# A kernel of Strassen-like passes: ScalarE copies four products of every unit, an accumulating transfer adds the former passes' sums, and VectorE makes all low halves

## The chip, the cores and the metric

The kernel runs on one core of a Trainium2 chip. The metric is the device time of one execution in microseconds; lower is better. The names of the engines in the profile are PE (TensorE), PEld (TensorE's weight loads), DVE (VectorE), ACT (ScalarE), POOL (GpSimd) and SP (SyncE, which here only issues DMAs).

## The reference

The input x has 8 batches of 512 rows and 2048 columns, all float32. Each batch goes through a linear layer with a low-rank adapter chosen by its id, then through a second linear layer whose weight is stored as 4-bit codes with a scale for each block of 64, and is added to the result:

```python
x = x + ffn(cond(x, weight, bias, lora_a, lora_b, scaling, adapter_id), codes, absmax, bias2)
# cond: x @ weight.T + bias + scale * (x @ a_sel.T) @ b_sel.T     (rank 16)
# ffn:  y @ w.T + bias2,  w = NF4[codes] * absmax by blocks of 64
```

## The kernel before

**The first stage** (to about 912 us of the profile) dequantises the second weight, multiplies the two weights into one, and writes to DRAM the blocks and block sums of this combined weight (`wc_d`) and of x (`xc_d`). This stage is left as it is by the change.

**The product stage** is a fast matrix multiplication with seven products in place of eight, used on two levels. The outer level has seven passes (index `i`, order `OUTER`), each of which multiplies one outer combination of x with one of the weight. A pass has eight units (`QB`; unit number `u = 8*i + q`), one for each batch, and a unit has seven inner products (`k` from 0 to 6, order `INNER = A11, SS1, S2, S4, S3, A12, A22`). A product is 12 matrix multiplications of 128x512 in float32r, or 24 of half the width in the first four passes (`LOWS`), where 16 columns of the adapter are carried along. Every factor is split into a rounded high part and a low rest, hence three multiplications for each block.

**The weight factors** (`comb[f]`, seven buffers, two halves `c` each) stay for a whole pass. At the border between two passes all seven are replaced: SP issues the loads of factor k as soon as product k of the last unit is done (SS1 has a second buffer and is loaded earlier), ACT rounds each half (`comb_hi`, L1001), and then the rest is made (`comb_lo`). DVE makes the rests of SS1, A11, S2, S4 and S3 (L1324) at the steps that `LO_STEPS` gives by hand; POOL makes those of A12 and A22 (L906). PE waits at the first unit of a pass for both halves of a factor before its product.

**The x factors** are made for every unit: SP loads `xg` (one buffer, L587) for unit u+1 at the top of unit u, when DVE has finished the low halves of unit u. DVE makes four sums of it (`sum_x`: L1355, L1358 at k = 2, L1361 at k = 3, L1363 at k = 4), ACT rounds (L1016), DVE subtracts (`x_lo`, L1374), two at k = 3, two at k = 4, three at k = 5. The low-rank columns go the same way through `a_br` and `a_b` (L1378, L1020, L1382, L1028), with one buffer.

**The sums.** The result of unit u is gathered in `r_sb[u % 2]`, four quarters. In passes 1 to 5 SP first loads the sums of an earlier pass into it (`load_base`, L594, issued at k = 1 of unit u-1 after a wait for the store from that buffer), and DVE adds all seven products to it from PSUM (`add_product`, L1452). In passes 0 and 6 (`fresh`) there is no such load: ACT copies the products `COPIED = (0, 1, 2, 6)` (L1063) and DVE adds the other three. The finished sums go to DRAM from SP (`store_sums`), to `m_d` or, in passes 4 and 5, to the output. In pass 6 the totals of two former passes are also loaded, DVE adds the low-rank product to them (`add_lora_pair`, L1465), and at the end of each unit the sums of all (`add_last` L1472, `add_second_last` L1478, 128x2048 each).

**Order.** All waits are semaphores written by hand; each engine runs its list in order. PE needs a PSUM bank free again (`evacuated`): before product 2 of a unit product 0 must have left, before 3 product 1, before 4 product 2, before 6 product 4. Within a step k, DVE's list is: the adaptor's small sums, `add_product`, the low-rank parts, `sum_x`, `x_lo`, and last `comb_lo`.

Of the kernel before, what the change touches and what calls it, by code (L numbers as in the profile page):

```python
# [6 lines left out]
def adaln_ffn_kernel(  # L7
# [29 lines left out]
    P = 128  # L37
# [137 lines left out]
    def fresh(u):  # L175
        return u < QB or u >= BOTH

    def adds_of(u):
        return 3 if fresh(u) else 8 if u >= LOWS else 7

    def added(u, k):
        before = sum(adds_of(n) for n in range(u))
        if fresh(u):
            return before + k - 2
        return before + k + 1 + (1 if u >= LOWS and k > 4 else 0)

    def copied(u, k):
        return 4 * (u if u < QB else QB + u - BOTH) + COPIED.index(k) + 1

    def lows_before(u):  # L190
        return sum(2 if n < QB else 4 for n in range(u))

    def x_bank(u):
        return 2 + 3 * (u % 2) if u < LOWS else 2 + u % 2

# [7 lines left out]

    def low_load(u, t, m):
        return (2 * (u % 2) + t, (u - LOWS) // 2 + 1) if u < BOTH else (2 * m + t, QB + u - BOTH + 1)
# [3 lines left out]

    BY_GPSIMD, ON_VECTOR = (A12, A22), 10  # L210
# [7 lines left out]
    def half_at(i, f, c):  # L218
        n = halves_of(i).index((f, c)) + 1
        if i and f in BY_GPSIMD:  # L220
            return 4 * (i - 1) + n - ON_VECTOR
        return 2 * NF + ON_VECTOR * (i - 1) + n if i else n
# [18 lines left out]
    LO_STEPS = {-1: [0], 0: [1], 2: [2], 3: [3], 5: [4], 6: [5, 6], 7: [7, 8], 8: [9]}  # L241
# [30 lines left out]
    with ctx:  # L272
# [62 lines left out]
        a_br = at("a_br", 59, [P, 2, 3, QT, R], F32)  # L335
# [74 lines left out]
        s_clo_p = sem("block_low_by_gpsimd")  # L410
# [16 lines left out]
        s_ab = sem("a_b_loaded")  # L427
# [17 lines left out]
        s_rld = [sem(f"base_loaded{i}") for i in range(2)]  # L445
        s_rst = [sem(f"sum_stored{i}") for i in range(2)]
        s_tld = [sem(f"total_loaded{i}") for i in range(2)]
# [20 lines left out]
        def _(sp):  # L468
# [141 lines left out]
            def out_block(q, t, m, h):  # L610
                row = tile_row(q, t, m)
                return o_rows[row:row + P, :].rearrange("p (j c) -> p j c", c=SW)[:, :, h * HW:(h + 1) * HW]

            def store_sums(u, t):
# [3 lines left out]
                elif fresh(u):  # L618
                    sp.wait_ge(s_add, added(u, 4))
                    sp.wait_ge(s_cpy, copied(u, 6))  # L620
                else:
                    sp.wait_ge(s_add, added(u, 6))
                src = r_sb[u % 2][:, t, :, :]
                if i < FINAL:
                    sp.dma_start(m_d[i, q, :, t, :], src.rearrange("p n o -> p (n o)")).then_inc(s_rst[u % 2], 16)
                else:
                    sp.dma_start(out_block(q, t, i - FINAL, 0), src.rearrange("p n (c o) -> p (n c) o", c=2)
                                 ).then_inc(s_rst[u % 2], 16)
# [1266 lines left out]
```

## Time and profile before

| | |
|---|---|
| median of 3 runs | 2107.86 us (2107.43 to 2111.29) |
| the profiled execution | 2105.49 us, of which its span is 2103.7 us |
| mean granted clock of TensorE | 0.985 |
| PE busy in the span | 2016.7 us (96%) |
| DVE, ACT, POOL busy | 1610.5 us (77%), 883.8 us (42%), 118.9 us (6%) |
| DMA | 526.14 MB, mean 250 GB/s |
| time of POOL's rests (L906) | 72.1 us in 24 instructions |

The profile's times are those of one execution on the one core. The busy time of PE is made of matrix multiplications that overlap, so it shows whether PE stood still, and not how fast it was. DMA share 1.00 means that all 16 DMA engines had work all the time. A stretch is given in us from the span's start.

### The profile page before, as it was taken

Reading aid. Unit: us, or ns where it says so; the run is one execution under the profiler, and the core shown is the slowest. Engines: PE = TensorE matmul, PEld = TensorE weight load, DVE = VectorE, ACT = ScalarE, POOL = GpSimd, SP = SyncE. Lnnn points to the kernel's source line nnn. Section 1 sums busy time; section 2 is a strip of 40 time slices with the busy share of each in tenths; the row PEclk is TensorE's granted clock in tenths of the full one; section 3 lists DMA queues with packets and bytes.
Section 4 is the critical chain, followed back from the end, with each engine's and each line's share of the span. In section 5 each row is a group of like instructions: output and inputs, shape, how many; then the busy total and the mean of one; then the engine's idle time right before and its main releaser. Section 6 shows DMA issues by size and latency. Waiting matters only on the chain.

```text
span 2103.7 us, 29439 instructions
## 1 busy us (share of the span) xinstructions
PE 2016.7 (96%) x10880; PEld 1713.2 (81%) x10880; DVE 1610.5 (77%) x2377; ACT 883.8 (42%) x1417; POOL 118.9 (6%) x79
## 2 busy tenths in 40 slices
PE   4899999999999999989999999989999999998997
PEld 4788778788878777889989989989997887886876
DVE  8899879866996465575577787787778778778887
ACT  8655555554555332343442342243242234234332
POOL 5100000000000000000020020020002002002000
PEclk8999999999999999999999999999999999999999
DMA  9778878887888788856478677786877878877876
GB/s 283 244 239 263 256 250 259 254 253 244 264 266 252 244 264 275 256 190 218 166 262 269 217 263 257 250 282 210 271 259 231 275 253 261 260 234 242 279 257 231
DMA packets 406277, 526.14 MB, mean 250 GB/s; under 512 B 22992, under 2 KB 293024, under 8 KB 406008
## 3 DMA queue, kind: packets, MB, share of 16 engines
q1 hardware_dynamic: 402824, 513.23, 75.6%
q0 software_dynamic: 3312, 11.03, 1.6%
q8 instruction: 88, 1.44, 0.3%
q14 instruction: 53, 0.43, 0.1%
HBM read 336.47 MB, written 188.76 MB: 250 GB/s over the span
## 4 chain that ended last, share of the span: by engine, by line
PE 80%; DVE 8%; DMA 5%; issue 3%; SPq 2%; ACT 1%; DVEq 0%; ACTq 0%
PE big L1638 19%; PE big L1640 19%; PE big L1639 19%; PE big L1826 10%; PE big L1824 10%; PE big L1653 2%; DVE comb L1324 2%; DMA rq<-xc_d 1%; PE big L1634 1%; DMA xc_d<-rq 1%; DMA a_br<-a_sel_d 1%; DMA comb_raw<-wc_d 1%; DVE r_sb L1452 1%; DMA code_w<-in_L_ffn_codes_dram 1%; DVE xs L1374 1%
## 5 line engine op out<-in xcount | busy, mean ns | idle before, releaser
L1824 PE MATMUL big<-comb,xs 128*128 128x256 f32 x1920 | 468.9, 282 | 15.0 <-DVE r_sb L1452 13.8
L1638 PE MATMUL big<-wq,tile 128*128 128x512 f32 x1088 | 468.4, 431 | 1.2 <-DVE tile L1259 1.2
L1826 PE MATMUL big<-comb,xs 128*128 128x272 f32 (+1 forms) x1920 | 468.0, 286 | 0.0
L1640 PE MATMUL big<-wq,tile 128*128 128x512 f32 x1088 | 427.2, 393 | 0.0
L1639 PE MATMUL big<-wq,tile 128*128 128x512 f32 x1088 | 426.3, 392 | 0.0
L1824 PEld LDWEIGHTS big<-comb,xs 128*128 128x128 f32 x1920 | 363.9, 190 | 20.1 <-DVE comb L1324 14.7
L1826 PEld LDWEIGHTS big<-comb,xs 128*128 128x128 f32 x1920 | 363.9, 190 | 2.3
L1638 PE MATMUL big<-comb,xs 128*128 128x512 f32 x832 | 332.3, 399 | 21.5 <-DVE r_sb L1452 14.8
L1452 DVE TENSOR_TENSOR r_sb<-big,r_sb 128x512 f32<-128x512 f32 x328 | 225.6, 688 | 149.7 <-PE big L1640 98.5
L1640 PE MATMUL big<-comb,xs 128*128 128x512 f32 x832 | 330.6, 397 | 0.0
L1639 PE MATMUL big<-comb,xs 128*128 128x512 f32 x832 | 330.4, 397 | 0.0
L1638 PEld LDWEIGHTS big<-wq,tile 128*128 128x128 f32 x1088 | 205.3, 189 | 68.0 <-ACT cs L968 3.5
L1640 PEld LDWEIGHTS big<-wq,tile 128*128 128x128 f32 x1088 | 204.9, 188 | 44.9
L1639 PEld LDWEIGHTS big<-wq,tile 128*128 128x128 f32 x1088 | 206.7, 190 | 25.5 <-issue 1.0
L1638 PEld LDWEIGHTS big<-comb,xs 128*128 128x128 f32 x832 | 158.3, 190 | 59.6 <-DVE comb L1324 21.3
L956 ACT CAST tile<-raw 128x1024 fp32r<-128x1024 f32 x136 | 141.7, 1053 | 119.7 <-DMA raw<-in_L_cond_weight_dram 117.7
L1016 ACT CAST xs<-xr 128x512 fp32r<-128x512 f32 x224 | 135.1, 619 | 131.0 <-DVE xr L1363 59.2
L1259 DVE TENSOR_TENSOR tile<-raw,tile 128x1024 fp32r<-128x1024 f32 x136 | 162.2, 1221 | 34.8 <-ACT tile L956 34.5
L1640 PEld LDWEIGHTS big<-comb,xs 128*128 128x128 f32 x832 | 158.2, 190 | 36.4
L1639 PEld LDWEIGHTS big<-comb,xs 128*128 128x128 f32 x832 | 158.4, 190 | 34.9
L906 POOL TENSOR_TENSOR comb<-comb_raw,comb 128x1024 fp32r<-128x1024 f32 x24 | 72.1, 3037 | 1661.1 <-ACT comb L1001 1661.1
L1374 DVE TENSOR_TENSOR xs<-xr,xs 128x512 fp32r<-128x512 f32 x224 | 148.9, 685 | 2.5 <-ACT xs L1016 1.9
(144 smaller groups left out, 2440.7 us busy)
## 6 DMA issues: line engine op xcount, KB each, us to landing
raw<-in_L_cond_weight_dram SPq DMA_DIRECT2D x128, 512.0 KB, 4.5
xg<-xc_d SPq DMA_DIRECT2D x112, 512.0 KB, 5.3
xc_d<-rq SPq DMA_DIRECT2D x26, 1792.0 KB, 7.6
r_sb<-m_d SPq DMA_DIRECT2D x80, 512.0 KB, 4.9
m_d<-r_sb SPq DMA_DIRECT2D x64, 512.0 KB, 6.1
wc_d<-cs SPq DMA_DIRECT2D x31, 896.0 KB, 4.9
tb<-wc_d SPq DMA_DIRECT2D x107, 256.0 KB, 5.0
x_nat<-in_x_dram SPq DMA_DIRECT2D x104, 256.0 KB, 4.0
```

Of the source, the lines that this page charges most:

```text
L906: tt(cw[f][:, ks, LO, 0:SW], cr[f][:, ks, LO, 0:SW], cw[f][:, ks, HI, 0:SW].bitcast(F32), ALU.subtract).then_inc(s_clo_p, 1)
L956: nc.scalar.copy(tile[slot][:, HI, :, :], raw[slot][:, LO, :, :]).then_inc(s_hi, 1)
L1016: nc.scalar.copy(x_slot(u, f)[:, HI, :, :], src).then_inc(s_xhi, 1)
L1259: tt(tile[slot][:, LO, :, :], raw[slot][:, LO, :, :], tile[slot][:, HI, :, :].bitcast(F32), ALU.subtract).then_inc(s_lo, 1)
L1324: tt(comb(i, f)[:, ks, LO, 0:SW], src, comb(i, f)[:, ks, HI, 0:SW].bitcast(F32), ALU.subtract).then_inc(s_clo, 1)
L1374: tt(x_slot(u, f)[:, LO, :, :], src, x_slot(u, f)[:, HI, :, :].bitcast(F32), ALU.subtract).then_inc(s_xlo, 1)
L1452: tt(dst, main(bank, u, k not in (1, 3)), dst, ALU.add).then_inc(s_add, 1)
L1638: nc.tensor.matmul(out_ap, t_hi, m_hi, start=first, stop=False, skip_group_check=onto)
L1639: nc.tensor.matmul(out_ap, t_hi, m_lo, start=False, stop=False, skip_group_check=onto)
L1640: return nc.tensor.matmul(out_ap, t_lo, m_hi, start=False, stop=last, skip_group_check=onto)
L1824: nc.tensor.matmul(big[:, bank, 0:HW], x, w[:, 0:HW], start=begin, stop=end, skip_group_check=not opens)
L1826: ins = nc.tensor.matmul(big[:, bank + 1, 0:wide], x, w[:, HW:HW + wide], start=begin, stop=end, skip_group_check=not opens)
```

## The change

Five things are done at once.

1. ACT copies products 0, 1, 2 and 6 of every unit, DVE adds 3, 4 and 5 onto the copies. The small copy `u_low` also goes from DVE to ACT.
2. `load_base` is gone. When a unit of passes 1 to 5 is complete, POOL issues for each half of `r_sb` a DMA that adds `m_d`'s sums to it (`accum_op=ALU.add`), waits for it, and issues the store, which SP issued before. `r_sb[u % 2]` is free for unit u+2 after these stores; ACT's copy of product 0 waits for that.
3. DVE makes the rests of A12 and A22 as well: four more halves for each border, by `LO_STEPS` at k = 1, 2, 3 and 4 of the first unit, each as the last thing of its step. POOL does no arithmetic in the product stage.
4. `a_b` and `a_br` have two buffers, and their load comes one unit earlier.
5. In the very last unit the low-rank pairs come earlier (at k = 3 and 4), one total has a buffer of its own, and the last sums are made and stored in three pieces, so that after the last product only 128x512 twice is left.

```diff
-    BY_GPSIMD, ON_VECTOR = (A12, A22), 10
-    LO_STEPS = {-1: [0], 0: [1], 2: [2], 3: [3], 5: [4], 6: [5, 6], 7: [7, 8], 8: [9]}
+    LO_STEPS = {-1: [0], 0: [1], 2: [2], 3: [3], 5: [4], 6: [5, 6], 7: [7, 8], 8: [9, 10], 9: [11], 10: [12], 11: [13]}
...
+        total_end = at("total_end", 176, [P, 2, 2, SW], F32)
-        a_b = at("a_b", 59, [P, 2, 3, QT, R], F32R)
+        a_b = [at(f"a_b{i}", kb, [P, 2, 3, QT, R], F32R) for i, kb in enumerate((59, 57))]
...
-            def load_base(u):
-                i, q = divmod(u, QB)
-                sp.wait_ge(s_rst[u % 2], 32 * (u // 2))
-                for t in range(2):
-                    sp.dma_start(r_sb[u % 2][:, t, :, :].rearrange("p n o -> p (n o)"), m_d[BASE_OF[i], q, :, t, :]
-                                 ).then_inc(s_rld[u % 2], 16)
...
@@ load_a(u) @@
-                if u:
-                    sp.wait_ge(s_aside, len(WITH_LOW) * u)
+                if u >= 2:
+                    sp.wait_ge(s_aside, len(WITH_LOW) * (u - 1))
...
@@ SP, top of unit u @@
+                if u and u + 2 < LOWS:
+                    load_a(u + 2)
                 if u + 1 < NU:
                     sp.wait_ge(s_xlo, NF * (u + 1))
                     load_x(u + 1)
-                if 1 <= u <= BOTH:
+                if 1 <= u <= QB:
                     store_sums(u - 1, 1)
...
@@ SP, step k of unit u @@
-                    if k == 1 and QB <= u + 1 < BOTH:
-                        load_base(u + 1)
...
-                if u < BOTH:
+                if u < QB:
                     store_sums(u, 0)
...
@@ POOL @@
-            for i in range(1, NF):
-                for n in range(ON_VECTOR, 2 * NF):
-                    f, c = halves_of(i)[n]
-                    ks = slice(HALF * c, HALF * (c + 1))
-                    pool.wait_ge(s_chi, 2 * NF * i + n + 1)
-                    tt(cw[f][:, ks, LO, 0:SW], cr[f][:, ks, LO, 0:SW], cw[f][:, ks, HI, 0:SW].bitcast(F32),
-                       ALU.subtract).then_inc(s_clo_p, 1)
+            for u in range(QB, BOTH):
+                i, q = divmod(u, QB)
+                if u < QB + 2:
+                    pool.wait_ge(s_rst[u % 2], 32 * (QB // 2))
+                else:
+                    pool.wait_ge(s_rst2[u % 2], 32 * ((u - QB) // 2))
+                for t in range(2):
+                    if t == 0:
+                        pool.wait_ge(s_add, added(u, 5))
+                    else:
+                        pool.wait_ge(s_cpy, copied(u, 6))
+                    pool.dma_start(r_sb[u % 2][:, t, :, :].rearrange("p n o -> p (n o)"), m_d[BASE_OF[i], q, :, t, :],
+                                   accum_op=ALU.add).then_inc(s_base[u % 2][t], 16)
+                for t in range(2):
+                    pool.wait_ge(s_base[u % 2][t], 16 * ((u - QB) // 2 + 1))
+                    src = r_sb[u % 2][:, t, :, :]
+                    if i < FINAL:
+                        pool.dma_start(m_d[i, q, :, t, :], src.rearrange("p n o -> p (n o)")
+                                       ).then_inc(s_rst2[u % 2], 16)
+                    else:
+                        pool.dma_start(out_block(q, t, i - FINAL, 0), src.rearrange("p n (c o) -> p (n c) o", c=2)
+                                       ).then_inc(s_rst2[u % 2], 16)
...
@@ ACT, copy_product(u, 0) @@
+                    elif u >= QB + 2:
+                        act.wait_ge(s_rst2[u % 2], 32 * ((u - QB) // 2))
...
@@ ACT, step k of unit u @@
-                    if k == 0 and u < QB:
+                    if k == 0 and u < LOWS:
                         copy_low(u)
-                    if fresh(u) and k in COPIED:
+                    if k in COPIED:
                         copy_product(u, k)
...
@@ DVE, add_product(u, k) @@
-                if fresh(u):
-                    dve.wait_ge(s_cpy, copied(u, 2))
-                elif k >= 3 and k < 6:
-                    dve.wait_ge(s_add, added(u, {3: 2, 4: 1, 5: 0}[k]))
-                else:
-                    dve.wait_ge(s_rld[u % 2], 32 * ((u - QB) // 2 + 1))
+                dve.wait_ge(s_cpy, copied(u, {3: 2, 4: 1, 5: 0}[k]))
...
+            def add_end(n):
+                u = NU - 1
+                t, cols = TAIL[n]
+                if t == 0:
+                    dve.wait_ge(s_add, added(u, 5))
+                    dve.wait_ge(s_cpy, copied(u, 2))
+                    dve.wait_ge(s_lev, 4 * QB)
+                elif cols.start == 0:
+                    dve.wait_ge(s_cpy, copied(u, 6))
+                first, both, out = (b[:, t, cols, :] for b in (total[u % 2], total_end, r_sb[u % 2]))
+                tt(first, first, out, ALU.add).then_inc(s_end, 1)
+                dve.wait_ge(s_end, 2 * n + 1)
+                tt(out, both, out, ALU.add).then_inc(s_end, 1)
...
+                    if u == NU - 1 and k in (3, 4):
+                        for n in range(2 * (k - 3), 2 * (k - 2)):
+                            add_lora_pair(u, n)
+                    if u == NU - 1 and k == 5:
+                        add_end(0)
+                        add_end(1)
+                    if u == NU - 1 and k == 6:
+                        add_end(2)
```

## Rows read from the trace of the kernel before

**Rows 1.** Windows, product stage; us, busy time by engine, clock, DMA share, GB/s.
```profile
...
1060.00:1085.00 25.00, 20.05 (x133) 18.64 (x132) 22.64 (x27) 15.24 (x22) 11.90 (x4) 0.93 0.88 315
1085.00:1225.00 140.00, 140.00 (x1014) 132.90 (x1013) 99.62 (x182) 39.11 (x88) 0.00 (x0) 1.00 0.72 240
...
1560.00:1592.00 32.00, 26.93 (x143) 22.53 (x142) 30.49 (x34) 18.17 (x25) 12.71 (x4) 0.95 0.96 320
...
1905.00:1940.00 35.00, 27.74 (x109) 21.48 (x108) 26.96 (x30) 18.35 (x25) 10.98 (x4) 0.90 0.72 245
...
912.00:2092.00 1180.00, 1144.40 (x6720) 1009.72 (x6719) 902.65 (x1348) 409.76 (x753) 72.11 (x24) 0.99 0.74 246
...
```

**Rows 2.** Waits of the weight loads, 912 to 2104 us; total, times, longest.
```profile
...
PEld big L1638 <- DVE comb L1324: 19.0, 6, 5.0
...
```

**Rows 3.** Timeline of PE, first border; start, length, instruction, [idle before].
```profile
...
1081.57 0.55 PE L1824 MATMUL big<-comb,xs 128*128 128x256 f32 x1 [4.95 <-DVE r_sb L1452]
...
```

**Rows 4.** Timeline of DVE, the same stretch.
```profile
...
1070.50 2.35 DVE L1324 TENSOR_TENSOR comb<-comb_raw,comb 128x1024 fp32r<-128x1024 f32 x2
...
1075.54 1.99 DVE L1378 TENSOR_TENSOR a_br<-a_br 128x64 f32<-128x64 f32 x1 [2.08 <-DMA a_br<-a_sel_d]
1077.45 3.37 DVE L1324 TENSOR_TENSOR comb<-comb_raw,comb 128x1024 fp32r<-128x1024 f32 x1
...
```

**Rows 5.** Timeline of POOL, the same stretch.
```profile
...
1071.14 11.90 POOL L906 TENSOR_TENSOR comb<-comb_raw,comb 128x1024 fp32r<-128x1024 f32 x4 [871.54 <-ACT comb L1001]
```

**Rows 6.** Timeline of SP's queue, second border.
```profile
...
1231.48 1.18 SPq L569 DMA_DIRECT2D comb_raw<-wi_d  x2
...
1233.82 1.22 SPq L587 DMA_DIRECT2D xg<-xc_d  x2
...
1245.61 0.80 SPq L594 DMA_DIRECT2D r_sb<-m_d  x2
```

**Rows 7.** Tile xg, 1225 to 1250 us: its two loads at that border.
```profile
...
DMA to landing us min/median/max: 8.5/9.2/10.0
```

**Rows 8.** Windows inside the second border.
```profile
...
1216.00:1222.00 6.00, 6.00 (x40) 5.41 (x39) 2.98 (x7) 0.82 (x2) 0.00 (x0) 1.00 1.04 370
...
1240.00:1243.00 3.00, 3.00 (x17) 2.47 (x15) 1.23 (x2) 1.21 (x2) 3.00 (x2) 1.00 1.02 412
...
```

**Rows 9.** DMA issues by line: count, size, median us to landing.
```profile
...
r_sb<-m_d SPq DMA_DIRECT2D x80, 512.0 KB, 4.9
m_d<-r_sb SPq DMA_DIRECT2D x64, 512.0 KB, 6.1
...
xc_d<-x_early POOLq DMA_DIRECT2D x12, 512.0 KB, 6.7
...
```

**Rows 10.** Timeline of DVE in the middle of a pass.
```profile
...
1140.36 0.69 DVE L1452 TENSOR_TENSOR r_sb<-big,r_sb 128x512 f32<-128x512 f32 x1 [2.06 <-PE big L1826]
...
1141.24 0.69 DVE L1355 TENSOR_TENSOR xr<-xg 128x512 f32<-128x512 f32 x1
1142.03 0.69 DVE L1358 TENSOR_TENSOR xr<-xr,xg 128x512 f32<-128x512 f32 x1
...
1143.73 0.68 DVE L1361 TENSOR_TENSOR xr<-xg,xr 128x512 f32<-128x512 f32 x1
1144.33 0.68 DVE L1374 TENSOR_TENSOR xs<-xg,xs 128x512 fp32r<-128x512 f32 x1
...
1160.30 0.69 DVE L1452 TENSOR_TENSOR r_sb<-big,r_sb 128x512 f32<-128x512 f32 x1 [0.93 <-PE big L1826]
...
```

**Rows 11.** Timeline of DVE at the end of the kernel.
```profile
...
2092.61 2.28 DVE L1472 TENSOR_TENSOR total<-total,r_sb 128x2048 f32<-128x2048 f32 x1
...
2096.13 2.29 DVE L1478 TENSOR_TENSOR r_sb<-total,r_sb 128x2048 f32<-128x2048 f32 x1
```

**Rows 12.** Chain that ended last, 2085 to 2104 us; start, length, what.
```profile
...
2091.20 0.24 PE big L1848
...
```

**Rows 13.** Timeline of SP's queue, last border.
```profile
...
1910.64 1.23 SPq L569 DMA_DIRECT2D comb_raw<-wi_d  x2
...
1920.23 1.42 SPq L587 DMA_DIRECT2D xg<-xc_d  x2
...
```

**Rows 14.** Timeline of ACT, last border.
```profile
...
1919.27 0.58 ACT L1063 COPY r_sb<-big 128x512 f32<-128x512 f32 x1
...
1929.33 0.62 ACT L1016 CAST xs<-xg 128x512 fp32r<-128x512 f32 x1 [3.50 <-DMA xg<-xc_d]
...
```

**Rows 15.** Timeline of PE, last border.
```profile
...
1919.99 0.76 PE L1638 MATMUL big<-comb,xs 128*128 128x512 f32 x1 [4.60 <-ACT r_sb L1063]
...
```

More of the change, by code:

```diff
@@ L173, in group_at, with pair_at @@
         return m, r, p, c
-    def fresh(u):
-        return u < QB or u >= BOTH
     def adds_of(u):
-        return 3 if fresh(u) else 8 if u >= LOWS else 7
+        return 4 if LOWS <= u < BOTH else 3
     def added(u, k):
-        before = sum(adds_of(n) for n in range(u))
-        if fresh(u):
-            return before + k - 2
-        return before + k + 1 + (1 if u >= LOWS and k > 4 else 0)
+        return sum(adds_of(n) for n in range(u)) + k - 2 + (1 if LOWS <= u < BOTH and k > 4 else 0)
     def copied(u, k):
-        return 4 * (u if u < QB else QB + u - BOTH) + COPIED.index(k) + 1
+        return 4 * u + COPIED.index(k) + 1
     def lows_before(u):
-        return sum(2 if n < QB else 4 for n in range(u))
+        return sum(2 if n < QB else 3 for n in range(u))
     def x_bank(u):
         return 2 + 3 * (u % 2) if u < LOWS else 2 + u % 2
+    def pair_at(u, n):
+        m, t = divmod(n, 2)
+        return (1 - m, t) if u == NU - 1 else (m, t)
+    TAIL = ((0, slice(0, 2)), (1, slice(1, 2)), (1, slice(0, 1)))
     def z_bank(u):
@@ L426, in adaln_ffn_kernel @@
         s_cpy = sem("product_copied")
-        s_ab = sem("a_b_loaded")
+        s_ab = [sem(f"a_b_loaded{i}") for i in range(2)]
         s_adf = sem("a_b_difference_made")
@@ L840, in _ @@
                             load_low(u + 1, t, m)
-            for m in range(2):
-                store_total(NU - 1, m)
+            for n, (t, cols) in enumerate(TAIL):
+                for m in range(2):
+                    sp.wait_ge(s_end, 2 * n + m + 1)
+                    src = (r_sb[(NU - 1) % 2] if m else total[(NU - 1) % 2])[:, t, cols, :]
+                    sp.dma_start(out_block(QB - 1, t, m, 1)[:, 2 * cols.start:2 * cols.stop, :],
+                                 src.rearrange("p n (c o) -> p (n c) o", c=2)).then_inc(s_out[m], 16)
             for n in range(2):
-                sp.wait_ge(s_rst[n], 32 * (BOTH // 2))
-                sp.wait_ge(s_out[n], 32 * QB)
+                sp.wait_ge(s_rst[n], 32 * (QB // 2))
+                sp.wait_ge(s_rst2[n], 32 * ((BOTH - QB) // 2))
+                sp.wait_ge(s_out[n], 32 * (QB - 1) + 16 * len(TAIL))
         @block.gpsimd
@@ L1019, in a_hi @@
                 act.wait_ge(s_adf, u + 1)
-                nc.scalar.copy(a_b[:, HI, :, :, :], a_br[:, LO, :, :, :]).then_inc(s_abhi, 1)
+                nc.scalar.copy(a_b[u % 2][:, HI, :, :, :], a_br[u % 2][:, LO, :, :, :]).then_inc(s_abhi, 1)
             def place_a(u, f):
@@ L1376, in a_difference @@
             def a_difference(u):
[L1377 to L1378 removed]
+                low, high, apart = (a_br[u % 2][:, LO, h, :, :] for h in range(3))
+                dve.wait_ge(s_ab[u % 2], 16 * (u // 2 + 1))
+                tt(apart, high, low, ALU.subtract).then_inc(s_adf, 1)
             def a_lo(u):
                 dve.wait_ge(s_abhi, u + 1)
[L1382 removed]
+                tt(a_b[u % 2][:, LO, :, :, :], a_br[u % 2][:, LO, :, :, :], a_b[u % 2][:, HI, :, :, :].bitcast(F32),
                    ALU.subtract).then_inc(s_ablo, 1)
@@ L1775, in evacuated @@
             def evacuated(u, k):
[L1776 removed]
+                if k in COPIED:
                     pe.wait_ge(s_cpy, copied(u, k))
@@ L1790, in multiply @@
                 if q == 0:
-                    pe.wait_ge(s_clo_p if i and f in BY_GPSIMD else s_clo, max(half_at(i, f, c) for c in range(2)))
+                    pe.wait_ge(s_clo, max(half_at(i, f, c) for c in range(2)))
                 if u < LOWS and f in WITH_LOW:
```

91 lines of the change are left out of this document (42 added, 49 removed).

## The prediction

> **What bounds the kernel now.** I read the windows of the product stage first, since the change touches nothing before it. In the middle of a pass PE is busy all the time: 140.0 of 140 us, at clock 1.00, with DVE at 99.6 us and ACT at 39.1 us of it [rows 1]. A unit takes 1160.30 - 1140.36 = 19.94 us there, a product 2.85 us [rows 10]. So nothing that ACT or DVE saves in mid-pass moves the end. From 912 to 2092 us PE stands still for 1180 - 1144.4 = 35.6 us, and the windows that lie over the borders show where: 4.95 us in the first, 5.07 in the fourth, 7.26 in the last [rows 1]; the other three read alike, and the six have some 33 us. After such a wait the granted clock falls from 2.4 to 1.2 GHz for a while: the first border's window has a mean of 0.93, which is 0.07 x 25 = 1.8 us more [rows 1]. Then comes the tail: the last matmul ends at 2091.4 us, DVE at 2098.4, the span at 2103.7 [rows 11, 12].
>
> Next, why PE waits at a border. The weight loads wait for DVE's rests, 19.0 us in six waits on one of the lines alone [rows 2]; at the first border it is one wait of 4.95 us, before the product with S3 [rows 3]. DVE's own timeline has the reason. Two halves take it 2.35 us in a row, but the next one takes 3.37 us and a small difference 1.99 us, after a wait of 2.08 us for `a_br` [rows 4]. These long ones lie inside POOL's four subtractions from 1071.14 to 1083.04 us [rows 5]: both engines are slow while both work. So today's stall is DVE's, made longer by POOL.
>
> **The change, term by term.**
>
> *Mid-pass.* Four additions less on DVE (0.60 us each from start to start, as 1143.73 to 1144.33 in rows 10) and four copies more on ACT: hidden under PE both ways, 0. ACT has 101 of 140 us free. The copy of product 0 is needed before product 2 begins, 2.85 us after product 0 ends, and takes 0.58 us [rows 14]. 0.
>
> *DVE at a border.* Gone are POOL's grip (1.17 us for a half where rows 4 show 3.37), the wait for `a_br`, and 4 x 0.60 = 2.4 us of additions per unit; new are four halves, 4 x 1.17 = 4.7 us. The S3 half that stops PE today will be ready in time. I read this as: the stall of today goes. What is late next? In DVE's list the second half of A22 now stands last in k = 4 of the first unit, behind `sum_x` and `x_lo` for the next unit, and these wait for `xg`. At the second border the unit begins at about 1231.5 (SP's load of A22 waits for the end of product 6), SP issues xg in two parts from 1233.82 [rows 6], and they take up to 10.0 us to land [rows 7]: 1234.4 + 10.0 = 1244.4, that is 12.9 us into the unit. From there DVE has, by the distances of rows 4 and 10: two sums 1.4, second half of A12 1.17, the addition 0.6, a sum 0.6, two `x_lo` 1.2, first half of A22 1.17, small parts 0.1, the addition 0.6, a sum 0.6, two `x_lo` 1.2, second half of A22 1.17; sum 9.8 us. So A22 is complete 22.7 us into the unit, and PE wants it at 6 x 2.85 = 17.1. A stall of 5.6 us, in the place of today's 5. In passes 4 and 5 `add_lora` stands in that list too: 6.3 us.
>
> *What the transfers do to that landing.* The DMA engines are full around a border: share 1.04 at 1216 to 1222 and 1.02 still at 1240 to 1243 us, at 370 to 412 GB/s [rows 8]. Ahead of xg in that burst stand today the base load of the coming unit (2 x 512 KB) and half of the last unit's store (512 KB). After the change they are gone from SP's queue, but the stores of the unit before come later and fall into the burst (1 MB), and the two accumulating transfers of the last unit stand in it at its worst moment. No row has an accumulating transfer. Lower bound: the load of the same size, 4.9 us; upper bound: a load and a store one after the other, 4.9 + 6.1 = 11.0 us, since it has to read `r_sb` besides writing it [rows 9]. A plain transfer of POOL's takes 6.7 [rows 9]. So the burst ahead of xg changes by +0.5 MB (priced as a load) to +1.5 MB (twice that): at 387 GB/s, the mean between 370 and 412 rounded down, 1.4 to 4.1 us later. I take 2, since a part of POOL's queue will still be running after xg. A gain is possible too, see the rivals. In the first border there is no accumulating transfer yet, and the base load of unit 8 is gone: 1.05 MB / 387 GB/s = 2.7 us earlier, stall 5.6 - 2.7 = 2.9 us.
>
> What would a page make of it? The Trainium skill, "DMA: Bandwidth & Descriptors", section "Rules for kernel authors", says that an accumulating DMA reads its destination and writes it later. By that rule the upper of the two prices is the nearer, and the borders would cost 2 us each more than I write; no row here can show it.
>
> *The last border.* PE stops for 4.60 us for ACT's copy, which comes at 1919.27, and resumes at 1919.99 [rows 14, 15]; before the copy ACT's list holds roundings whose loads SP issued as late as 1910.64 [rows 13]. The change leaves this as it is. xg is issued at 1920.23 [rows 13] and used at 1929.33 after a wait [rows 14]; + 9.8 is 1939.1. Without a further wait PE would reach product 6 at 1920.0 + 4 x 2.85 + 1.7 (low clock) = 1933.1. So 4.6 + 6.0 = 10.6 us, and 1 for the fuller DMA: 11.6, where today it is 7.3 [rows 1].
>
> *Sum of the borders*: 2.9 + 2 x 7.6 + 2 x 8.3 + 11.6 = 46.3 us against 33: +13. The low clock comes after each wait before and after: 0.
>
> *The r_sb buffer.* POOL's chain for a unit begins with the copy of product 6, 0.7 us after the unit's end: accumulate, store (6.1), two issues of about 1 us. ACT wants the buffer 19.94 + 2.85 = 22.8 us after that end, so the accumulation may take 22.8 - 0.7 - 2 - 6.1 = 14 us. Both bounds (4.9 and 11.0) fit: 0, with the price below if not.
>
> *SP* issues less (0.8 us for two base loads, [rows 6]) and waits less; it is not what PE waits for in mid-pass: 0.
>
> *The tail.* Today, after the last matmul: 2.28 + 1.15 + 2.29 us of additions with their gaps, end at 2098.4, and 5.3 us to the end of the span [rows 11]. Afterwards: a copy of 0.6, two additions of 0.6 and 0.7, so the end at 2091.4 + 2.0 = 2093.4, and 5.0 for a smaller store: 2098.4. -5.3 us.
>
> Sum: +13 - 5.3 = +7.7 us on the profiled execution's own 2105.5, 2113.2. The median of the runs shown lies 2.4 us above that execution, so 2115.6; I say 2115.
>
> **The rivals.**
>
> *A, faster: SP's queue gets through sooner.* xg stands behind 1.5 MB less in its own queue. If POOL's transfers take little from the engines while SP's queue is full, xg lands up to 1.55 MB / 387 GB/s = 4 us earlier, and the stalls become 2.9, 2 x 1.6, 2 x 2.3 and about 8: 19 us, so -14, and stalls under 3 us may keep the clock: about -5. With the tail -24: 2083. For it: DVE is free of POOL, and the median landing of POOL's plain transfers, 6.7, is slow. Against: full DMA engines [rows 8] serve both queues. The Trainium skill, "DMA: Bandwidth & Descriptors", section "Queues, rings and completion order", has each DMA engine take turns between the queues that have work; by that POOL's part comes at once and A gets nothing.
>
> *B, no difference: the accumulation costs as little as the load.* Then xg lands as today: 2.9 + 2 x 5.6 + 2 x 6.3 + 10.6 = 37.3, +4, less the tail 5.3: -1, 2107.
>
> *C, much slower: the accumulation is longer than 14 us.* Then ACT's copy of product 0 waits for POOL's store, and ACT holds up PE in mid-pass too. It decides from 14 us for ACT and 17 for PE; at 23 us it would cost (23 - 17) / 2 = 3 us for each of about 38 units, +114: 2220. Both bounds speak against it.
>
> **How the numbers follow.** Forecast 0.42 (2109 to 2126), A 0.30, B 0.20, C 0.08. A measurement of this kernel tells about 0.2% (4.2 us) from no change. Faster by more: A and a little of B, 0.34. Within: most of B and the lower edge of the forecast, 0.22. Slower: 0.44. The range takes in A down to 2080 and the forecast with the price of the accumulation doubled again (five borders by 4 us) up to 2145; half of A's low side and C are outside, under 0.2.
>
> **What would show it.** In the trace after: PE without idle time in mid-pass; at each border one wait, no longer before S3 but before A22 (product 6), released by DVE's L1324 group, with DVE waiting for xg shortly before; halves at 1.22 us throughout; accumulating transfers of 5 to 11 us; xg landing 9 to 12 us after its issue; the span's end about 12.3 - 5.3 = 7 us behind the last matmul. The prediction is wrong if xg lands early (A), if ACT's copies wait for POOL's stores (C), or if DVE reaches k = 4 late for another reason than xg.

## Result, and the profile after

The changed kernel takes 2158.09 us (median; 2155.66 to 2159.74), the kernel before 2107.66 (2107.43 to 2111.29) beside it: ratio 1.0239, 95% interval 1.0227 to 1.0252. It is slower, as the forecast's sign had it, but by 50 us where the prediction had 8; the time is outside the range.

The page of the changed kernel, then windows of its product stage (busy time of PE, PEld, DVE, ACT, POOL, then clock, DMA share, GB/s):

```profile
PE 2035.0 (94%) x10880; PEld 1727.1 (80%) x10880; DVE 1495.2 (69%) x2221; ACT 975.5 (45%) x1601; POOL 167.6 (8%) x215
...
q1 hardware_dynamic: 367528, 429.33, 61.8%
q0 software_dynamic: 26352, 94.93, 17.2%
```

```profile
940.00:1060.00 120.00, 120.00 (x869) 113.92 (x869) 70.01 (x120) 47.94 (x106) 0.00 (x0) 1.00 0.60 199
1066.00:1096.00 30.00, 24.77 (x164) 23.34 (x163) 23.20 (x34) 16.38 (x28) 0.94 (x1) 0.89 0.56 189
1100.00:1210.00 110.00, 110.00 (x794) 104.27 (x793) 62.14 (x113) 41.43 (x95) 14.79 (x21) 1.00 0.82 244
1214.00:1268.00 54.00, 44.54 (x288) 41.41 (x288) 35.95 (x54) 26.69 (x47) 6.07 (x9) 0.91 0.77 237
...
1950.00:2000.00 50.00, 34.16 (x118) 25.95 (x117) 33.32 (x43) 22.53 (x31) 3.27 (x4) 0.83 0.67 222
912.00:2146.00 1234.00, 1161.01 (x6703) 1022.73 (x6703) 788.22 (x1188) 500.65 (x936) 120.96 (x160) 0.97 0.77 235
```

In the middle of pass 1 PE still never stops (110.00 of 110 us), though the DMA share is 0.82 where it was 0.72 [rows 1]: the moved copies and additions are hidden. From 912 us to the end of the stage PE stands still for 1234 - 1161.01 = 73.0 us, where it was 35.6, nearly all at the borders; a border's clock is 0.83 to 0.91, where it was 0.90 to 0.95 [rows 1]. By the trace's clock records the time at 1.2 GHz grows from 27.3 to 71.7 us, and half of each such us at most is lost: up to 22 us. The last matmul of the kernel before, then of the changed one:

```profile
2091.65 0.40 PE L1848 MATMUL big<-g_b,low_st 128*128 128x512 f32 x1
```

```profile
2149.70 0.39 PE L1669 MATMUL big<-comb,xs 128*128 128x512 f32 x1
```

It ends at 2092.05 and at 2150.09 us, 58.0 us later. Of these 37.4 are standing still, and 20.6 are PE longer busy with the same matmuls, which fits the low clock. The spans end 11.6 us (2103.7) and 7.5 us (2157.6) behind these ends: -4.1. Together +53.9, the distance of the spans.

**The first border.** PE's timeline, then DVE's:

```profile
1082.78 0.39 PE L1853 MATMUL big<-comb,xs 128*128 128x256 f32 x1 [1.22 <-DVE comb L1338]
...
1089.94 0.58 PE L1853 MATMUL big<-comb,xs 128*128 128x256 f32 x1 [4.00 <-DVE comb L1338]
```

```profile
1074.01 2.35 DVE L1338 TENSOR_TENSOR comb<-comb_raw,comb 128x1024 fp32r<-128x1024 f32 x2
1076.81 0.36 DVE L1397 TENSOR_TENSOR a_b<-a_br,a_b 128x192 fp32r<-128x192 f32 x1 [0.45 <-ACT a_b L1032]
1080.10 0.69 DVE L1369 TENSOR_TENSOR xr<-xg 128x512 f32<-128x512 f32 x1 [2.93 <-DMA xg<-xc_d]
...
1081.51 1.22 DVE L1338 TENSOR_TENSOR comb<-comb_raw,comb 128x1024 fp32r<-128x1024 f32 x1
...
1085.05 1.22 DVE L1338 TENSOR_TENSOR comb<-comb_raw,comb 128x1024 fp32r<-128x1024 f32 x1
...
1088.67 1.22 DVE L1338 TENSOR_TENSOR comb<-comb_raw,comb 128x1024 fp32r<-128x1024 f32 x1
```

This is the predicted wait at the predicted place: the stall before S3 [rows 3] is gone, halves take 1.22 us, and PE stops before product 6 until the last half of A22 (1088.67 + 1.22). Ahead of it DVE had stood still for `xg` for 2.93 us. Such a wait before product 6 stands at each of the six borders: 4.00, 3.21, 2.67, 5.14, 4.61 and 4.03 us, 23.7 in sum.

**The second border**, unit 15, the last of pass 1. From here on accumulating transfers run beside the burst. PE, ACT and DVE:

```profile
1235.85 0.55 PE L1853 MATMUL big<-comb,xs 128*128 128x256 f32 x1 [3.96 <-DVE r_sb L1457]
```

```profile
1228.96 1.05 ACT L1013 CAST comb<-comb_raw 128x1024 fp32r<-128x1024 f32 x1 [4.73 <-DMA comb_raw<-wc_d]
```

```profile
1230.05 1.23 DVE L1338 TENSOR_TENSOR comb<-comb_raw,comb 128x1024 fp32r<-128x1024 f32 x1 [4.02 <-ACT comb L1013]
1231.19 0.68 DVE L1457 TENSOR_TENSOR r_sb<-big,r_sb 128x512 f32<-128x512 f32 x1
...
1235.02 0.68 DVE L1457 TENSOR_TENSOR r_sb<-big,r_sb 128x512 f32<-128x512 f32 x1
```

This wait the prediction did not have. Read backwards: product 6 waits for the addition of product 4 (1235.02), which stands in DVE's list behind a rest of A11's weights, which waits for ACT's rounding, which waits for the load. PE also waits in the last units of passes 2 and 3 (4.56 and 5.24 us, there seen at the transposes on L1801). The rest of A11 waits for ACT there too, for 2.06 and 1.77 us, but the sums of `xg` ahead of it had waited for their load first, 2.10 and 8.98 us, so late loads of both kinds share in these. The wait comes, in those of passes 4 and 5 (1.90 and 2.01). The four parts of that load, from issue to landing, first in the kernel before, where they were issued from 1214.4 us:

```profile
L561 SPq DMA_DIRECT2D comb_raw<-wc_d x4: 370/510/1210, 1214.4 to 1216.7; - x4
...
DMA to landing us min/median/max: 4.7/5.6/6.6
```

and in the changed one, from 1217.7 us:

```profile
L563 SPq DMA_DIRECT2D comb_raw<-wc_d x4: 370/714/982, 1217.7 to 1219.7; - x4
...
DMA to landing us min/median/max: 9.6/10.2/10.9
```

What ran beside them is in POOL's timeline: two accumulating transfers issued just ahead. The stores behind them wait for their landing, so the first took at most 5.7 us and the second at most 11.1:

```profile
1213.51 0.87 POOL L909 DMA_DIRECT2D r_sb<-m_d  x1 [6.70 <-DVE r_sb L1457]
1215.74 0.87 POOL L909 DMA_DIRECT2D r_sb<-m_d  x1 [1.36 <-ACT r_sb L1077]
1219.17 0.56 POOL L915 DMA_DIRECT2D m_d<-r_sb  x1 [2.56 <-DMA r_sb<-m_d]
1226.87 0.54 POOL L915 DMA_DIRECT2D m_d<-r_sb  x1 [7.14 <-DMA r_sb<-m_d]
```

**The last border** has the longest stop. ACT's copy stands behind roundings that wait for late loads:

```profile
1971.30 0.76 PE L1667 MATMUL big<-comb,xs 128*128 128x512 f32 x1 [6.34 <-ACT r_sb L1077]
1977.75 0.47 PE L1667 MATMUL big<-comb,xs 128*128 128x512 f32 x1 [1.53 <-ACT r_sb L1077]
1986.39 0.50 PE L1667 MATMUL big<-comb,xs 128*128 128x512 f32 x1 [1.94 <-DVE comb L1338]
1993.47 0.80 PE L1667 MATMUL big<-comb,xs 128*128 128x512 f32 x1 [4.03 <-DVE comb L1338]
```

**All transfers**, by line: count, size, median us to landing.

```profile
xg<-xc_d SPq DMA_DIRECT2D x112, 512.0 KB, 6.8
...
r_sb<-m_d POOLq DMA_DIRECT2D x80, 512.0 KB, 8.3
...
m_d<-r_sb POOLq DMA_DIRECT2D x48, 512.0 KB, 7.0
comb_raw<-wi_d SPq DMA_DIRECT2D x44, 512.0 KB, 9.8
comb_raw<-wc_d SPq DMA_DIRECT2D x83, 256.0 KB, 8.8
```

Accumulating takes 8.3 us where the load took 4.9 [rows 9], and everything beside it lands later: xg 6.8 (5.3 before), the two kinds of loads of weights 9.8 and 8.8 (7.6 and 6.3 before).

### The profile page after: what moved, and what is told of

The parts are those of the page before. It is cut to its first block, busy times and chain, and to the rows that moved or that the text cites. A ratio compares the mean times of both kernels' runs of the same rounds, so it can differ in the third digit from the quotient of the medians.

```text
span 2157.6 us, 29402 instructions
## 1 busy us (share of the span) xinstructions
PE 2035.0 (94%) x10880; PEld 1727.1 (80%) x10880; DVE 1495.2 (69%) x2221; ACT 975.5 (45%) x1601; POOL 167.6 (8%) x215
## 3 DMA queue, kind: packets, MB, share of 16 engines
q0 software_dynamic: 26352, 94.93, 17.2%
## 4 chain that ended last, share of the span: by engine, by line
PE 73%; DMA 10%; DVE 9%; issue 3%; SPq 3%; ACT 1%; DVEq 0%; ACTq 0%
PE big L1667 18%; PE big L1669 18%; PE big L1668 18%; PE big L1855 7%; PE big L1853 7%; DMA xg<-xc_d 6%; PE big L1682 2%; DVE xs L1388 2%; DMA comb_raw<-wc_d 2%; DVE comb L1338 1%; DMA rq<-xc_d 1%; SPq L563 1%; PE big L1663 1%; DVE r_sb L1457 1%; DMA low_d<-low_st 1%
## 5 line engine op out<-in xcount | busy, mean ns | idle before, releaser
L1853 PE MATMUL big<-comb,xs 128*128 128x256 f32 x1920 | 479.0, 286 | 25.0 <-DVE comb L1338 13.4
L1855 PE MATMUL big<-comb,xs 128*128 128x272 f32 (+1 forms) x1920 | 477.2, 290 | 0.0
L1853 PEld LDWEIGHTS big<-comb,xs 128*128 128x128 f32 x1920 | 371.2, 193 | 30.1 <-DVE comb L1338 16.4
L1855 PEld LDWEIGHTS big<-comb,xs 128*128 128x128 f32 x1920 | 371.2, 193 | 2.4
L1077 ACT COPY r_sb<-big 128x512 f32<-128x512 f32 x224 | 131.6, 587 | 353.5 <-PE big L1669 213.0
L1667 PEld LDWEIGHTS big<-comb,xs 128*128 128x128 f32 x832 | 159.6, 192 | 72.6 <-DVE comb L1338 30.3
L1669 PEld LDWEIGHTS big<-comb,xs 128*128 128x128 f32 x832 | 159.5, 192 | 37.0
L1668 PEld LDWEIGHTS big<-comb,xs 128*128 128x128 f32 x832 | 159.8, 192 | 35.1
L1273 DVE TENSOR_TENSOR tile<-raw,tile 128x1024 fp32r<-128x1024 f32 x136 | 162.2, 1220 | 35.5 <-ACT tile L968 35.4
L909 POOL DMA_DIRECT2D r_sb<-m_d x80 | 70.3, 887 | 1312.4 <-DVE r_sb L1457 1241.7
```

What stands on the lines that cost most here:

```text
L909: pool.dma_start(r_sb[u % 2][:, t, :, :].rearrange("p n o -> p (n o)"), m_d[BASE_OF[i], q, :, t, :], accum_op=ALU.add).then_inc(s_base[u % ...
L1077: nc.scalar.copy(quarter_of(r_sb[u % 2], t, n), main(bank, u, k != 1)).then_inc(s_cpy, 1)
L1273: tt(tile[slot][:, LO, :, :], raw[slot][:, LO, :, :], tile[slot][:, HI, :, :].bitcast(F32), ALU.subtract).then_inc(s_lo, 1)
L1667: nc.tensor.matmul(out_ap, t_hi, m_hi, start=first, stop=False, skip_group_check=onto)
L1668: nc.tensor.matmul(out_ap, t_hi, m_lo, start=False, stop=False, skip_group_check=onto)
L1669: return nc.tensor.matmul(out_ap, t_lo, m_hi, start=False, stop=last, skip_group_check=onto)
```

## The experiments

Two questions: how much is the order of VectorE's list, how much are the transfers; and are the two independent? In e1, e2, e10 and e11 the kernel leaves out a part of the result, as each expectation says; they serve as measurements alone. Each run stood beside runs of the kernel before (medians 2107.0 to 2108.2); the ratios are to those. "Still" is PE's time without work from 912 us to the end of the stage, "low" the time at 1.2 GHz, of all clock records that reach into it, counted whole. Both are of the profiled execution, "us" is the median of all.

| run | us | ratio, 95% | still | low |
|---|---|---|---|---|
| before | 2107.7 | 1 | 35.6 | 27.3 |
| changed | 2158.1 | 1.0227 to 1.0252 | 73.0 | 71.7 |
| e1 plain load | 2134.1 | 1.0096 to 1.0145 | 60.6 | 58.0 |
| e2 no base | 2118.0 | 1.0021 to 1.0053 | 43.8 | 37.5 |
| e3 before, rests on VectorE | 2122.2 | 1.0042 to 1.0085 | 43.8 | 37.5 |
| e4 before, last unit changed | 2103.6 | 0.9973 to 0.9996 | 37.1 | 27.3 |
| e5 A22 early | 2122.6 | 1.0053 to 1.0093 | 50.4 | 44.4 |
| e6 and A11 late | 2128.0 | 1.0071 to 1.0112 | 54.6 | 34.1 |
| e7 old sums, two a_b | 2103.5 | 0.9967 to 0.9989 | 35.4 | 30.7 |
| e8 and rests on VectorE, early | 2097.8 | 0.9932 to 0.9967 | 29.7 | 37.5 |
| e9 lists eased | 2135.4 | 1.0103 to 1.0143 | 55.9 | 64.9 |
| e10 eased, plain load | 2103.1 | 0.9964 to 0.9990 | 35.0 | 37.5 |
| e11 eased, no base | 2082.8 | 0.9869 to 0.9900 | 20.1 | 20.5 |
| e12 old sums, eased | 2090.1 | 0.9901 to 0.9932 | 27.1 | 17.1 |

**e1 and e2: the transfers, in the changed kernel's own lists.** e1 drops `accum_op`; e2 drops the transfers of the former sums altogether.

```diff
                     pool.dma_start(r_sb[u % 2][:, t, :, :]..., m_d[BASE_OF[i], q, :, t, :],
-                                   accum_op=ALU.add).then_inc(s_base[u % 2][t], 16)
+                                   ).then_inc(s_base[u % 2][t], 16)
```

> The changed kernel with POOL's accumulating transfer replaced by a plain load of the same bytes into the same buffer at the same place (so it leaves out the sums of products 0 to 6 in passes 1 to 5: the load overwrites them). Theory P, price: the accumulation is dear for the DMA engines, and that delays the loads of the weight factors and of xg at the borders. Then a plain load gives back most of the 22 us of waits before the borders and their low clock: 2125 to 2140 us, and the transfer lands in about 5 us. Theory Q, place: base loads and stores now fall into the burst of loads before a border, whatever they cost. Then the time stays within 6 us of 2158, and the waits of PE in the last unit of a pass stay.

> The changed kernel without the accumulating transfers at all (it leaves out the former passes' sums); POOL only stores. Traffic falls by 42 MB. Theories P and Q both say that the waits before the borders (4.0, 4.6, 5.2, 1.9, 2.0 us before product 6 of a pass's last unit) mostly go: 2158 - 18 - about 12 of low clock = 2125 to 2135. The waits before products 5 and 6 of a pass's first unit come from the order in DVE's list (A22's rest behind sum_x, which waits for xg) and stay at 3 to 5 us each, so the kernel does not become faster than 2110. Rival: the copies on ACT are the cause; then the time stays above 2145.

The same bytes as plain loads at the same place: 24.0 us less. Without them another 16.1 less. So without the transfers of the former sums 40 of the 50 us are gone, more than was expected of e2. That counts them against none at all; what they cost against the loads of the kernel before follows from e3 and e4. The four parts of A11's load in unit 15 land in 7.3 to 8.2 us in e1 and 5.4 to 6.6 in e2, where the changed kernel had 9.6 to 10.9. The waits before product 6 of first units stay in e2, at five of six borders to the hundredth (4.00, 3.21, 2.67, 4.94, 4.61, 4.03): they are not the transfers'. The waits of the last units are gone. The share of POOL's queue says what the accumulation costs the engines; the page of e1:

```profile
q1 hardware_dynamic: 367528, 429.33, 62.7%
q0 software_dynamic: 26352, 94.93, 12.6%
```

17.2% of 2157.6 us against 12.6% of 2136.2 us: 102 us of 16 engines' time more for the same 94.93 MB, where 94.93 MB took 269.

**e3 and e4: two parts of the change on the kernel before.**

```diff
 # e3: GpSimd's loop of rests is gone
-    LO_STEPS = {-1: [0], ..., 7: [7, 8], 8: [9]}
+    LO_STEPS = {-1: [0], ..., 7: [7, 8], 8: [9, 10], 9: [11], 10: [12], 11: [13]}
 # e4: pair_at, TAIL, total_end, add_end and the stores of the last unit, as in the change
```

> The kernel before with one part alone: DVE makes the rests of A12 and A22 at the steps that the change gives, POOL none; base loads, additions and the rest as before. Theory L (list): the stall before S3 goes and one of 5 to 7 us before products 5 and 6 takes its place at each border, since these rests stand behind sum_x, which waits for xg: 2103 to 2116 us. Rival: only the fuller DMA of the changed kernel makes xg late, and with the traffic of before DVE free of POOL brings 3 us or more at each border: under 2092.

> The kernel before with the changed last unit alone (low-rank pairs at k = 3 and 4, one total in a buffer of its own, last sums in three pieces). Every theory: 4.8 us less, as the trace after shows at its end (7.5 us from the last matmul to the end of the span instead of 12.3): 2103.

e3 is 14.0 us slower than the runs beside it (14.5 above 2107.7), more than expected, with the waits before product 6 of the changed kernel (3.84, 3.21, 2.67, 5.02, 4.60, 4.04). e4 gives back 4.1 to 4.6. Added up they give 2107.7 + 14.5 - 4.1 = 2118.1 us for a kernel with both parts and the loads of before, and the changed kernel takes 40.0 more: that is an estimate of what the move of the sums costs in these lists. e2 has 2118.0, so the whole change without the former sums costs no more than these two parts. It does not show that the copies on ScalarE are free: e2 also has 42 MB less to move, and the two were not separated.

**e5: the order alone.** In a pass's first unit VectorE makes A22's rests before it turns to the next unit.

```diff
-... 8: [9, 10], 9: [11], 10: [12], 11: [13]}
+... 8: [9, 10, 11, 12, 13]}
```

> The changed kernel; in a pass's first unit VectorE makes the second half of A12's rest and both of A22's in k = 1, before a_lo, sum_x and x_lo of the next unit, and not in k = 2 to 4. Nothing of the transfers differs. Theory L (the wait before product 6 of a first unit is the place of A22's rests in VectorE's list, behind operations that wait for xg): the six waits of 4.0, 3.2, 2.7, 5.1, 4.6 and 4.0 us (23.7) and the 1 to 2 us before each go; two or three us a border are left elsewhere, and some of the low clock goes with them: 2125 to 2138. Theory T (A22's high part, or its load, comes late as well since accumulating transfers fill the engines; the place in the list is only where it is seen): VectorE then stands still in k = 1 for ScalarE, its additions of products 3 and 4 come late, and the waits stay within 30% in sum: 2150 to 2165. The waits of the last unit of a pass (4.0 to 5.2 us) stay by both.

35.5 us less than the changed kernel, from one line and with no transfer touched, a little more than expected. With the 40 of e2 this comes to more than the 50 between the two kernels, so the two causes share waits and do not add up. The six waits for A22's rest before product 6 are gone. What is left are the last units' waits and ScalarE's copy of product 2:

```profile
1232.35 0.36 PE L1853 MATMUL big<-comb,xs 128*128 128x256 f32 x1 [3.79 <-DVE r_sb L1457]
1250.37 0.54 PE L1853 MATMUL big<-comb,xs 128*128 128x256 f32 x1 [2.09 <-ACT r_sb L1077]
```

From the first product (at 898.4 us; in e5 at 903.2, its first stage took longer) to the end of the last matmul the profiled executions are 34.9 us apart: 24.8 of standing still, and 10.1 of PE busy with the same matmuls, which goes with 27.3 us less at 1.2 GHz. The clock is under a third of it.

**e6 and e9: moving the other waits by the lists.** e6 adds to e5 that A11's weights are rounded and their rests made one step later in the last unit. e9 instead leaves ScalarE's rounding of A11 where it is, moves only VectorE's part, spreads A22's rests, and rounds A22 behind the copy of product 2.

```diff
 # e6
-        if q == QB - 1 and i < LAST and k >= 2 and k != 3:     # A11 at k = 2
+        if q == QB - 1 and i < LAST and k >= 3:                # A11 at k = 3
-    LO_STEPS = {..., 2: [2], 3: [3], 5: [4], ...
+    LO_STEPS = {..., 3: [2], 4: [3], 5: [4], ...
 # e9: LO_STEPS as in e6, but 8: [9, 10, 11], and
-        if q == 0 and i and k < 2:                             # ScalarE: A12, A22 at k = 0, 1
+        if q == 0 and i and k in (0, 2):                       # at k = 0, 2
+                    if i and q == 0:                           # VectorE, ahead of a_lo and sum_x
+                        for n in {2: [12], 3: [13]}.get(k, ()):
+                            comb_lo(i, n)
```

> As the run before, and in the last unit of a pass ScalarE rounds A11's weights in k = 3 and not in k = 2, VectorE's rests of them in k = 3 and 4. Theory B (the wait of 4.0 to 5.2 us before product 6 of the last unit is additions 3 and 4 standing in VectorE's list behind a rest of A11, whose load takes 11 us beside the accumulating transfers): these waits (some 14 to 18 us in sum) go, the load has 2.85 us more: 2110 to 2125. Rival R (the load is later than that too, or the wait moves to the first products of the next pass, which need A11 and S2): less than 5 us under the run before, with new waits within the first 6 us of a pass. Were both lists harmless now, what is left above the run without base traffic with the same order would be the transfers' own.

> The changed kernel with its transfers as they are and three places of the lists eased: VectorE makes A22's rests of a first unit ahead of a_lo and sum_x, one in k = 2 and one in k = 3; the rests of A11 in the last unit one k later (k = 3 and 4) while ScalarE rounds them in k = 2 as now; ScalarE rounds A22 in k = 2, behind its copy of product 2, and not in k = 1. If what the lists do to the waits is all that the order can give back (theory L), the waits before product 6 of last units and the waits for ScalarE's copy of product 2 go and 2122.5 of the order alone becomes 2108 to 2116. If those waits are only where late loads are seen (theory T), the stall moves to another product of the same border: 2118 to 2126.

Neither gained. e9 is 12.8 us above e5 and outside both of its expectations. e6 is 5.5 us above it by the medians, but the intervals overlap, and from the first product to the last matmul the profiled executions take 1216.8 (e5) and 1216.9 us (e6): no difference is shown. In e6 the last units' waits go (of those of 4 to 5 us, 1.2 and 2.2 are left at two transposes), and in the next unit PE waits for ScalarE's copies of products 0 and 1 instead: 1.4 + 4.8 us at the second border, 9.1 at once at the last. ScalarE stands before a load there too, 4.20 us at the second border. That is rival R in kind. In e9 the wait in unit 15 is as long as ever (4.00 us), since VectorE now waits for `xs` of ScalarE, which stands still for the same load; and the half of A22 made in k = 3 stands behind the wait for `xg`, with the addition of product 4 behind it. VectorE, then PE:

```profile
1250.99 0.69 DVE L1370 TENSOR_TENSOR xr<-xg 128x512 f32<-128x512 f32 x1 [3.23 <-DMA xg<-xc_d]
```

```profile
1256.18 0.47 PE L1805 MATMUL big<-ident,low_rep 128*128 128x128 f32 x1 [3.77 <-DVE low_rep L1431]
1256.88 0.55 PE L1857 MATMUL big<-comb,xs 128*128 128x256 f32 x1 [0.22 <-DVE r_sb L1458]
```

So these waits, unlike A22's in e5, are where late loads are seen, and a list only chooses the place.

**e10 and e11: the eased lists of e9 with a plain load, and without the former sums.** The edits are those of e1 and e2.

> The run before with plain loads in place of the accumulating ones (the former sums are not added). In the late lists this was worth 24 us. If the accumulation costs PE only through loads that come late in the burst, and the eased lists cover them, the two runs are within 6 us; if the price is one that no list covers, 15 to 25 us less than the run before.

> The run before without any transfer of the former sums (they are not added). In the late lists this was worth another 16 us, and 40 in all. With the eased lists, by the first theory 2098 to 2106, within 10 us of the kernel with accumulating transfers; by the second 2080 to 2095.

32.3 us less, more than expected, then 20.3 less again: 52.6 us between e9 and e11, 40.1 between the changed kernel and e2. The eased list does not hide the transfers; more of their price is seen with it. Why more is not shown: VectorE's waits for xg fall about as far with either list, from 111.5 us (changed) to 37.0 (e2), and here, e9 and then e11 (us in total, times, longest):

```profile
DVE xr L1370 <- DMA xg<-xc_d: 118.7, 37, 8.4
```

```profile
DVE xr L1366 <- DMA xg<-xc_d: 31.7, 18, 4.1
```

And the lists of e9, poor with accumulating transfers, are good without them: 35.2 us less than e2.

**e7, e8 and e12: a version that beats both.** The kernel before with the changed last unit and two buffers for a_b (e7); all rests on VectorE too, five halves in k = 1 (e8); or these with the lists of e9, halves 11 and 12 in k = 2 and 13 in k = 3 ahead of a_lo (e12). SyncE loads the former sums and VectorE adds them, as before.

```diff
 # e8, on e7
-    LO_STEPS = {..., 8: [9]}
+    LO_STEPS = {..., 8: [9, 10, 11, 12, 13]}
 # e12, on e7
+    LO_STEPS = {-1: [0], 0: [1], 3: [2], 4: [3], 5: [4], 6: [5, 6], 7: [7, 8], 8: [9, 10]}
+    AHEAD = {2: [11, 12], 3: [13]}
```

> The kernel before with the changed last unit and two buffers for a_b; the sums of former passes, the copies and GpSimd's four rests stay as before. The last unit alone gave -4.6 us. The second buffer takes VectorE's wait for a_br (2.08 us at the first border) away in the time in which S3's rest is late. If that wait is a term of the stall before S3 (theory S), five borders are 1 to 2 us shorter and the time is 2092 to 2100; if VectorE's slow rests beside GpSimd alone set the stall (theory G), it is 2101 to 2105.

> As the run before, and VectorE makes all rests of A12 and A22, in k = 1 of a first unit before the next unit's operations (the order of the first run here); GpSimd makes none. Made in the late order alone this cost +14 us. Theory L with additions of its own hidden: the stalls before S3 and before A22 both go, 10 to 20 us less than the kernel before by them and 5 by the end: 2082 to 2096. Rival V (VectorE has too much in the first units with 7 additions each and four halves more; whatever stands late stalls): 2103 to 2118, with waits before products 2 to 4 of first units.

> The kernel before with the changed last unit, two buffers for a_b, all rests on VectorE, and the eased lists; the former sums are loaded by SyncE and added by VectorE as before. The version with all rests in k = 1 gave 2097.8 and had left a wait of 3.4 to 4.2 us at each border, where the addition of product 2 stood behind five halves. With only two halves ahead of that addition the wait goes: 2078 to 2090. If VectorE has no room (two halves a product and 7 additions), the wait moves on to product 3 or 4 and the time stays at 2094 to 2100.

e7 is e4 again: VectorE's waits for `a_br` fall from 7.5 to 0.3 us in all and the time stays, so the wait for `a_br` [rows 4] was no term of the old stall. e8 takes 5.7 us off that, less than expected, and waits 3.4 to 4.2 us at most borders for the addition behind the five halves. e12 is 0.84% faster than the kernel before (ratio 0.9916). Its windows:

```profile
912.00:2078.00 1166.00, 1138.95 (x6709) 1005.12 (x6708) 893.14 (x1373) 408.52 (x752) 0.00 (x0) 0.99 0.75 249
```

VectorE has room for all fourteen halves and seven additions a unit; 27.1 us of standing still are left, 5.4 of them ScalarE's copy at the last border.

These runs also price the move of the sums directly (accumulating transfers on GpSimd's queue and copies on ScalarE, in place of loads on SyncE's queue and additions), with the order of the rests the same: e5 is 24.8 us above e8, and e9 45.3 above e12 (half 11 stands one step apart there). With the 40.0 from e3 and e4 the price is 25 to 45 us, whatever the list. In the eased lists 32.3 of the 45.3 are the accumulation (e10), and some 13 are left for the later place and the copies together (e10 against e12).

## Why the prediction was wrong, point by point

*Mid-pass 0.* Right, apart from two stops of 1.24 and 1.22 us before transposes in pass 2.

*DVE at a border: the old stall goes, A22's second half is late behind xg.* Right in place, kind and order, and e5 shows the cause. The forecast had 2.9 us at the first border (4.00 + 1.22 measured) and 5.6 to 6.3 at the next ones (2.7 to 5.1 at product 6, with 1.0 to 1.8 us more for half 11 ahead of it). But the size was too low: by the forecast's own terms the borders without slower transfers come to 37.3 us against 33, +4, and on the kernel before this part costs 14 us (e3), of which 8.2 are standing still. Its reading that the wait for `a_br` belonged to the old stall was wrong (e7). But A22's wait does not follow xg as I had it: it is the same in e2 and in the changed kernel, though xg lands at 5.6 us there and 6.8 here. At the first border DVE has 7.2 us of work in a row from the end of half 11 to that of half 13, and PE one product, 3.2 us at the clock of that moment: once half 11 is late the difference, 4.0 us, follows whole. It is less where PE also has transposes in between (3.21, 2.67), and more where `add_lora` stands in DVE's list (5.14, 4.61). When xg lands moves only the wait ahead of it, before product 5.

*What the transfers do to that landing: 2 us a border.* This is the step that failed, and by itself it holds most of the miss: it put 9 us into the sum (46.3 against 37.3), and the move costs 25 to 45 us, about 40 in these lists. The volume ahead of xg was counted; the loads of A11 to A22 in the same burst were not. Those of A11 at the second border land in 10.2 us where it was 5.6, and product 6 of the last unit, the copies on ScalarE and `low_st` wait for them. The accumulation costs 24 us above the same bytes as plain loads at the same place (e1), and those 16 above none (e2). The upper price, 11.0 us for one accumulating transfer, was there in the text; it was met at unit 15 (10.8 us), and the longest took 11.8, though the median is 8.3. Of the rise from 4.9 to 8.3 the later place in the burst has 2.0 us, since the plain load there takes 6.9 (e1), and the accumulation 1.4. The Trainium skill, "DMA: Bandwidth & Descriptors", section "Rules for kernel authors", says that an accumulating DMA reads its destination and writes it later; the traces agree in direction, with 8.3 us against 6.9. (In the working, 387 GB/s is called the mean of 370 and 412, which is 391; no term moves by more than 0.1 us.)

*The last border, 11.6.* Too low: 6.34 + 1.53 + 1.94 + 4.03 = 13.8 us in its first unit, after 2.01 in the one before.

*The low clock, 0.* Wrong: 44 us more of it, and PE is busy 20.6 us longer. Before there was one dip for each border; now there are two or three from the second border on. It was set at nothing because a dip follows each wait before and after; the number of waits was what changed.

*The r_sb buffer, 0.* Right: no stop of PE in mid-pass came from it, ACT never waits for POOL's stores in the trace, and the longest accumulation is 11.8 us, under the 14.

*The tail, -5.3.* Right in kind, a little high: -4.1 (the span now ends 7.5 us behind the end of the last matmul, where it was 11.6; e4 alone gives 4.1 to 4.6). The 2091.4 of the working is not the last matmul's end: that matmul starts at 2091.65. The 12.3 us of the working, and of e4's expectation, come from it.

*The rivals.* A fell: xg lands later, not earlier. Nor do stalls under 3 us always keep the clock, as it had hoped: behind single stops of 1.90 us (at 1776.0) and 2.01 us (at 1954.6) the granted clock is 0.50 at 1778 to 1780 and at 1955.5 to 1958 us. The Trainium skill, "DMA: Bandwidth & Descriptors", section "Queues, rings and completion order", has each DMA engine take turns between the queues that have work, and the trace agrees in so far as SP's loads beside POOL's transfers land in 10.2 us where it was 5.6. B fell with e1. C did not come about; the time between the forecast and C belonged to no case.

What stays open: e1 takes away the read of the destination but leaves the issue, the queue and the waits; whether the 24 us come from the engines' time alone or from the longer landing that POOL's store waits for was not separated. The copies on ScalarE were never run apart from the transfers. The dips of the clock were counted, not controlled.

## What to carry to other kernels

Where an engine issues from a list written out by hand, an operation that waits for a load holds everything behind it: put what is already possible ahead of it, and count how much work lies between two things that another engine needs one after the other. One line of that kind was worth 35 us here, beside the heavy transfers; on the kernel with the old loads the late order costs about 20 (2118.1 by e3 and e4, against 2097.8 in e8). When a transfer is moved or made heavier, price it by every load in the busiest stretch, not only by the one on the path: DMA engines with a mean share of 0.74 had nothing to spare in the bursts that set the end.

## What the runs showed of the hardware

An accumulating transfer of 512 KB took 8.3 us (median) where a plain load at the same place and queue took 6.9, and the longest 11.8; POOL's queue took 17.2% of the engines' span where plain loads took 12.6%. That is 102 us of 16 engines' time more for the 80 accumulating transfers, 1.3 us for each. Without these transfers the queue took 6.9% of 2116.2 us (e2); so, if the stores cost the same in all three runs, an estimate is 1.5 us of 16 engines' time for a plain load of 512 KB and 2.8 for an accumulating one. And its neighbours pay as much as itself: loads of weights from 8.6 and 7.0 us (e1) to 9.8 and 8.8. What PE pays for a stop is more than the stop: from e5 to the changed kernel, 24.8 us more of standing still came with 27.3 us more at 1.2 GHz and 10.1 us more of PE busy with the same matmuls.
